# Neighbour sums tile by tile, gate logits with the gate matrix stationary, and one GpSimd split behind a new wait

## The reference, cut to what matters

```python
def _L1_gnn_ref(x, wc, wn, bias, edge_index):      # second layer
    alpha = x @ wc
    beta = x @ wn
    sums = segment_sum(beta[dst], src)
    return alpha + sums / counts[:, None] + bias

def _L2_gnn_ref(x, gate_W, gate_b, Wl, bl, Wr, edge_index):   # third layer
    gates = softmax(x @ gate_W + gate_b)            # 4 experts
    top_v, top_i = top_k(gates, 2)
    # each of 4 experts, two layers:
    #   h = relu(mean_over_neighbours(h) @ Wl[e, l] + bl[e, l] + h @ Wr[e, l])
    # out = the two chosen experts, weighted by their gates
```

## Time and profile before

| what | value |
|---|---|
| median of 3 runs | 498.01 us (497.74 to 500.13) |
| the profiled execution, its own time | 497.47 us |
| its span, first to last instruction | 495.7 us |
| outside the span | 1.8 us |
| PE busy | 458.0 us, 92% |
| DVE busy | 306.9 us, 62% |
| ACT busy | 192.0 us, 39% |
| POOL busy | 164.2 us, 33% |
| chain that ended last, by engine | PE 63%, DVE 20%, issue 6%, POOL 5%, ACT 3%, DVE queue 3% |

### The profile page before, as it was taken

One profiled execution on the slowest core, in us unless ns is written; L12 is line 12 of the kernel. 1 busy time (PEld: TensorE's weight loads), 2 busy tenths in 40 slices (PEclk: granted clock), 3 DMA queues, 4 the chain that ended last, 5 costly groups with the idle time before them and its releaser, 6 DMA issues.

```text
span 495.7 us, 5939 instructions
## 1 busy us (share of the span) xinstructions
PE 458.0 (92%) x2107; PEld 334.1 (67%) x2107; DVE 306.9 (62%) x574; ACT 192.0 (39%) x264; POOL 164.2 (33%) x107
## 2 busy tenths in 40 slices
PE   4999996889869899899899999999999999999996
PEld 2465442334346778678678888888888888888654
DVE  5999836999975994877685333622362237133654
ACT  5888516546130631142441335123422252224232
POOL 3000131112243984448150433443344334343000
PEclk9999999899979999889998999999999999999999
DMA  8750000000030224203220032203420242120002
GB/s 265 202 225 1 1 1 22 0 1 0 1 106 0 72 100 170 85 1 117 77 86 0 19 127 110 86 2 109 161 87 3 91 141 89 41 85 1 0 1 85
DMA packets 22474, 34.34 MB, mean 69 GB/s; under 512 B 5680, under 2 KB 5936, under 8 KB 22448
## 3 DMA queue, kind: packets, MB, share of 16 engines
q1 hardware_dynamic: 22160, 33.85, 20.2%
q10 hardware_dynamic: 288, 0.13, 0.1%
HBM read 32.93 MB, written 1.05 MB: 69 GB/s over the span
## 4 chain that ended last, share of the span: by engine, by line
PE 63%; DVE 20%; issue 6%; POOL 5%; ACT 3%; DVEq 3%; DMA 1%; POOLq 0%
PE ps L1146 16%; PE ps L1148 16%; PE ps L1147 16%; PE ps L1208 4%; DVE one_src L784 3%; PE ps L1174 3%; PE ps L1175 3%; DVE rsum L886 2%; DVEq L784 2%; DVE e_sb L373 2%; DVE stats L713 2%; POOL x_sb L477 1%; PE ps L1287 1%; POOL w_lo L453 1%; PE ps L1159 1%
## 5 line engine op out<-in xcount | busy, mean ns | idle before, releaser
L452 POOL TENSOR_TENSOR w_lo<-w_stage,w_hi 128x1024 fp32r<-128x1024 f32 x22 | 52.7, 2395 | 137.7 <-ACT w_hi L528 137.7
L528 ACT ACTIVATE w_hi<-w_stage 128x2048 fp32r<-128x2048 f32 x23 | 43.9, 1910 | 73.1 <-PE ps L1148 73.1
L453 POOL TENSOR_TENSOR w_lo<-w_stage,w_hi 128x1024 fp32r<-128x1024 f32 x22 | 57.4, 2607 | 0.0
L1146 PE MATMUL ps<-w_hi,hid_hi 128*128 128x512 f32 x128 | 49.8, 389 | 0.0
L1147 PE MATMUL ps<-w_lo,hid_hi 128*128 128x512 f32 x128 | 49.8, 389 | 0.0
L1148 PE MATMUL ps<-w_hi,hid_lo 128*128 128x512 f32 x128 | 49.8, 389 | 0.0
L1063 DVE TENSOR_SCALAR tmp<-ps,bl 128x512 f32<-128x512 f32 x16 | 12.0, 751 | 52.2 <-ACT hid_hi L670 52.2
L1146 PE MATMUL ps<-T_hi,w_hi 128*128 128x512 f32 (+1 forms) x112 | 41.6, 372 | 1.8 <-DVE T_lo L743 1.4
L1148 PE MATMUL ps<-T_hi,w_lo 128*128 128x512 f32 (+1 forms) x112 | 40.7, 363 | 0.0
L1147 PE MATMUL ps<-T_lo,w_hi 128*128 128x512 f32 (+1 forms) x112 | 40.7, 363 | 0.0
L471 POOL TENSOR_TENSOR rstd<-vareps,scalars 128x1 f32<-128x1 f32 x24 | 15.8, 660 | 59.4 <-DVE vareps L715 59.4
(11 more groups left out here) (206 smaller groups left out, 1064.4 us busy)
## 6 DMA issues: line engine op xcount, KB each, us to landing
w_stage<-in_L_gnn_Wr SPq DMA_DIRECT2D x8, 1024.0 KB, 5.3
w_stage<-in_L_gnn_Wl SPq DMA_DIRECT2D x8, 1024.0 KB, 5.2
w_stage<-in_L_gnn_W SPq DMA_DIRECT2D x5, 1024.0 KB, 6.3
x_sb<-in_x SPq DMA_DIRECT2D x4, 256.0 KB, 3.6
w_q<-in_L_gnn_Wq SPq DMA_DIRECT2D x1, 1024.0 KB, 7.8
w_k<-in_L_gnn_Wk SPq DMA_DIRECT2D x1, 1024.0 KB, 10.1
w_v<-in_L_gnn_Wv SPq DMA_DIRECT2D x1, 1024.0 KB, 5.7
w_o<-in_L_gnn_Wo SPq DMA_DIRECT2D x1, 1024.0 KB, 9.6
```

The source lines that it names most:

```text
L452: gp.tensor_tensor(w_lo[s][:, 0:2], stage[s][:, 0:2], f32(w_hi[s][:, 0:2]), ALU.subtract)
L453: gp.tensor_tensor(w_lo[s][:, 2:4], stage[s][:, 2:4], f32(w_hi[s][:, 2:4]), ALU.subtract)\
L528: nc.scalar.activation(w_hi[u % 2][:], stage[u % 2][:], ACT.Copy).then_inc(hi_made, 1)
L1146: nc.tensor.matmul(goal, a_hi, b_hi, start=start, stop=False, **kw)
```

## The change

Three things change, and what they need.

1. The neighbour sums of the second layer are written out in place of the call: for each output tile all eight products k = 0 to 3 in a row, with the branch `If(slow > 0)` ahead of the last pair of each tile, so four branches in place of one.
2. The gate matrix, hi and lo side by side as 8 columns `gw`, becomes the stationary operand and T the moving one: 4 matmuls of T_hi into 8 rows of bank 3 and 4 of T_lo into its first 4 rows. ACT copies the 8 rows to SBUF (`gate_rows`). After the first two banks of expert 0's first product, PE turns them back with 4 matmuls in plain float32: `gate_rows` (8 rows, 128 columns) is stationary, and `fold`, an 8 x 4 matrix that adds the hi and lo rows, moves. DVE makes `fold` at the start by one small addition.
3. POOL waits for `tr_lo` of LN4's last tile before it splits the second expert matrix.

```diff
@@ gpsimd
             split_lo(FIRST_EXPERT)
             rstd_of(LN4)
+            gp.wait_ge(tr_lo, split_no(T4, NT - 1))
             for u in range(FIRST_EXPERT + 1, W_LAST + 1):
                 split_lo(u)
@@ scalar
                 nc.scalar.activation(agg_hi[:, j, :], tmp[:, j, :], ACT.Copy).then_inc(agg_hi_made, 1)
+            act.wait_ge(gate_rows_done, 1)
+            nc.scalar.activation(gate_rows[0:2 * EXPERTS, :], ps[0:2 * EXPERTS, 3, :], ACT.Copy)              .then_inc(gate_rows_out, 1)
             act.wait_ge(gexp_ask, 1)
@@ vector
-            link(nc.vector.tensor_copy(gw_hi[:], gate_w[:]))
-            nc.vector.tensor_tensor(gw_lo[:], gate_w[:], f32(gw_hi[:]), ALU.subtract).then_inc(gate_split, 1)
+            link(nc.vector.tensor_copy(gw_hi, gate_w[:]))
+            nc.vector.tensor_tensor(gw_lo, gate_w[:], f32(gw_hi), ALU.subtract).then_inc(gate_split, 1)
+            nc.vector.tensor_tensor(fold[:], ident[:, 0:EXPERTS], ident[:, EXPERTS:2 * EXPERTS], ALU.add)              .then_inc(gate_split, 1)
@@ tensor
-            sums_over_edges(0, ct_hi, ct_lo, R_hi, R_lo, beta_lo_made, 0, 1, gamma_done)
+            for t in range(NT):
+                for k in range(NT):
+                    if k == NT - 1:
+                        with pe.If(slow > 0):
+                            for kk in range(NT):
+                                nc.tensor.matmul(ps[:, t, :], ct_lo[:, kk, col(t)], R_hi[:, kk, :], start=False,
+                                                 stop=False, skip_group_check=True)
+                    nc.tensor.matmul(ps[:, t, :], ct_hi[:, k, col(t)], R_hi[:, k, :], start=k == 0, stop=False)
+                    last = nc.tensor.matmul(ps[:, t, :], ct_hi[:, k, col(t)], R_lo[:, k, :], start=False,
+                                            stop=k == NT - 1)
+                last.then_inc(gamma_done, 1)
@@ tensor
-            pe.wait_ge(gate_split, 1)
-            for t in range(NT):
-                for k in range(DT):
-                    last = mm3(ps[:, 3, t * EXPERTS:(t + 1) * EXPERTS], T_hi[:, k, col(t)], T_lo[:, k, col(t)],
-                               gw_hi[:, k, :], gw_lo[:, k, :], k == 0, k == DT - 1)
-            last.then_inc(logits_done, 1)
+            pe.wait_ge(gate_split, 2)
+            for k in range(DT):
+                nc.tensor.matmul(ps[0:2 * EXPERTS, 3, :], gw[:, k, :], T_hi[:, k, :], start=k == 0, stop=False,
+                                 skip_group_check=True)
+            for k in range(DT):
+                last = nc.tensor.matmul(ps[0:EXPERTS, 3, :], gw_hi[:, k, :], T_lo[:, k, :], start=False,
+                                        stop=k == DT - 1, skip_group_check=True)
+            last.then_inc(gate_rows_done, 1)
@@ tensor, in the loop over the banks j of an expert's first layer
+                        if n == 0 and e == 0 and j == 2:
+                            pe.wait_ge(gate_rows_out, 1)
+                            for t in range(NT):
+                                last = nc.tensor.matmul(ps[:, 3, t * EXPERTS:(t + 1) * EXPERTS],
+                                                        gate_rows[0:2 * EXPERTS, col(t)], fold[0:2 * EXPERTS, :],
+                                                        start=t == 0, stop=t == NT - 1, skip_group_check=True)
+                            last.then_inc(logits_done, 1)
                         if n == 0 and e == 0 and j == 3:
                             pe.wait_ge(logits_out, 1)
```

More of the change, by code:

```diff
@@ L123, in build @@
     part = place("part", [P, NT, D], F32, rM)
+    gate_rows = place("gate_rows", [P, N], F32, rM)
+    fold = place("fold", [P, EXPERTS], F32, rM + N * 4)
     one_dst = place("one_dst", [P, RING, P], F16, rVZ)
@@ L162, in build @@
     gate_w = little("gate_w", [P, DT, EXPERTS])
-    gw_hi = little("gw_hi", [P, DT, EXPERTS], F32R)
-    gw_lo = little("gw_lo", [P, DT, EXPERTS], F32R)
+    gw = little("gw", [P, DT, 2 * EXPERTS], F32R)
+    gw_hi, gw_lo = gw[:, :, 0:EXPERTS], gw[:, :, EXPERTS:2 * EXPERTS]
     scalars = little("scalars", [P, 2])
@@ L312, in build @@
         gate_split, logits_done, logits_out = sem("gate_split"), sem("logits_done"), sem("logits_out")
+        gate_rows_done, gate_rows_out = sem("gate_rows_done"), sem("gate_rows_out")
         gexp_ask, gexp_done = sem("gexp_ask"), sem("gexp_done")
```

## The result

| | median of the runs | lowest to highest | ratio to before, 95% interval |
|---|---|---|---|
| before | 498.01 us | 497.74 to 500.13 (5 runs) | |
| the change | 495.27 us | 494.05 to 495.71 (5 runs) | 0.9929 [0.9906, 0.9951] |
| the change, again beside other kernels (e5) | 495.34 us | 493.88 to 497.50 (12 runs) | 0.9940 [0.9921, 0.9959] |

The account below looks back on a forecast made before the run. TensorE, gapless from the expert phase on, was taken as the bound, so earlier starts reach the end. 1.60 + 3.62 + 1.55 - 2.0 - 0.81 = 3.96 us less: 498.01 to 494.1 us, range 491.9 to 496.0.

Parts of the forecast that it names:

- The ladder: TensorE's waits for R_lo of each tile, from gamma to the logits: sums' order and moved split together gain 1.60 us.
- The sums tile by tile: Neighbour sums ahead of the first normalisation: R_lo of the first tile 0.34 us earlier, bounds 0 and 1.36.
- That rival: Branches between gamma's tiles stop TensorE's issue; at 2.5 us each the kernel takes 500.5 us; chance 0.04.
- The logits: Gate logits on TensorE: eight matmuls of 512 columns take 1.81 us in place of 5.43, 3.62 gained.
- The new wait: TensorE ahead of bank 2 waits for ACT's copy `gate_rows`, behind `agg_lo` blocked by the split: 2.0 us lost.
- The fold: Four plain-float matmuls ahead of bank 2 that turn the logits back: 0.81 us lost, between 0.4 and 1.0.
- The clock: TensorE's clock was to stay at 1.00 throughout; a fall in the gap ahead of bank 2 had chance 0.12.
- mine lies near the first: The 2.8 us gap ahead of bank 2 resembles an earlier 2.64 us stretch of transposes that stayed at clock 1.00.
- The likeliest case: The whole-kernel forecast: 3.96 us less, 494.1 us, with 493.1 to 494.6 from its unknown sizes; chance 0.60.
- the clock's rival: The clock falls in the gap ahead of bank 2, eight products take 1.55 us more: 495.6 us; chance 0.12.
- The chances: Whole-kernel time: faster than 495.5 us 0.79, within 0.5% 0.16, slower 0.05.

Follow-up runs that it names:

- e5: The change itself, run and profiled once more beside other kernels: 495.34 us, ratio 0.9940.
- e4: The kernel before with only GpSimd's (POOL's) new wait added, so the split of the second expert matrix moves down: 498.31 us, ratio 1.0003.
- e3: The change without GpSimd's new wait, so the split runs at its old place: 493.29 us, ratio 0.9899.
- e7: The kernel before with only the neighbour sums' edit (tile by tile): 497.09 us, ratio 0.9984.
- e6: The kernel before with only the logits' edit: 492.04 us, ratio 0.9872.
- e1: The change with ACT's copy of the logit rows moved from behind the fourth `agg_hi` to behind the second: 491.48 us, ratio 0.9864.
- e2: The change with eight useless matmuls of 512 columns put ahead of TensorE's wait for the copy: 492.80 us, ratio 0.9889.
- e8: e1 with ACT's wait for gamma moved from ahead of the first normalisation to behind it: 489.96 us, ratio 0.9827.
- e10: e8 without GpSimd's new wait, so the split is back at its old place: 491.87 us, ratio 0.9870.
- e11: The change with sixteen useless matmuls of 4 columns ahead of TensorE's wait for the copy: 495.35 us, ratio 0.9939.
- e9: The change with four useless matmuls of 512 columns ahead of TensorE's wait for the copy: 495.37 us, ratio 0.9930.

## Why the prediction was right and where it failed

**The ladder** was right: 1.94 us gained in place of 1.60. Of these the new wait gave 1.6 (e4: 20.67 - 19.09; e3), where the forecast's share was 1.26. The first block came at 9.71 as laid out (9.72); the last two steps were 2.33 and 2.29 instead of 2.47 once R_lo was ready well ahead.

**The sums tile by tile**, 0.34 us: right in size in e7 (0.31 at n = 1), for the reason given, ACT's wait for all four tiles. The queue ahead of the first R_lo went; but e6 shows that it hung on 0.4 us by which DVE starts late in the kernel before, and that beside the logits' edit this order of the sums is worth nothing. The added branches cost nothing: 32 matmuls from 235.29 to 242.32 are 0.227 apart. That rival is out. The small addition that makes `fold` delayed nothing late, as forecast, but it wasn't small: it reads two operands in SBUF beside a split of POOL and lasted 2.42 us (227.41 to 229.83, where POOL's half ends at 229.80). The last addition of alpha still starts 0.20 us after gamma's first matmul, as before.

**The logits** were right: 1.85 us in place of 1.81 (254.02 to 255.87). So these matmuls with 8 and 4 stationary columns start as far apart as those with 128, 0.23 us.

**The new wait** was right: TensorE went on 28.02 us after gamma, forecast 28.33, and waited 1.96 us (263.31 less 261.35, where the next matmul would have started), forecast 2.0. The Trainium skill (SBUF — State Buffer, "Who interferes with whom") says that a VectorE instruction with two SBUF inputs contends with a GpSimd one that reads SBUF, that the port pair they share is an exclusive lock, and that the order of issue decides who blocks; here the trace agrees, with 1.74 and 1.50 us for `agg_lo` where 0.69 is usual.

**The fold** was too cheap: 0.98 us in e1, e2 and e5, where the clock is at 1.00 while it runs, in place of 0.81. In the change's first profile it took 1.25, above the bound of 1.0; the granted clock over these 1.25 us is 0.76: there the fall begins within it, in e5 behind it.

**The clock** is where the forecast failed. The step was "mine lies near the first": I judged the 2.8 us ahead of bank 2 by one stretch in one profile, and gave the fall 0.12 and a price of 1.55 us. It fell in both profiles of the change, for 1.6 and 3.2 us; with the rival's own price, 34.6 + 1.55 = 36.15 us is where e5 has its n = 1. The likeliest case was thus the wrong one (its own span was 493.1 to 494.6 us). The median, 495.27, is that of the clock's rival (495.6), and it lies within the range (491.9 to 496.0) because the range reached to that rival: the number held, the path to it did not. The gap without dense matmuls is the cause: the granted clock is 0.50 behind it in both profiles of the change, and it is 1.00 where the wait is gone (e1, e3, e6, e8, e10) or filled with dense matmuls (e2). The stretch that I compared it with was no safe measure either, for in e11 the clock fell there. The Trainium skill (TensorE: Matmul & The Clock Gate, "Why this matters for your kernels") warns of idle gaps between matmul bursts, but only of gaps longer than this one, a condition that the prediction left out. The traces go against it as a bound: the clock fell behind 1.81 us of idle time in the change and behind 0.91 us in e9's profile.

**The chances**: faster by over 0.5% had 0.79. The median fell 2.74 us, 0.55%, which is just over the bound of 2.5 us; the interval of the ratio, 0.9906 to 0.9951, reaches to just inside half a per cent. With the fall of the clock missed, that the median fell on this side of the bound is in part luck.

## What to carry to other kernels

Moving work out of one queue's way puts it in another's: look which late consumer stands behind the new place, and in which order its engine serves it; here one copy, served two places too late, turned a gain of 1.6 us into a loss of 2. A wait of TensorE costs its length and what the clock loses behind it: here 2.0 us and then 1.6 or 3.2 more. Place a wait that can't be avoided where dense matmuls can cover it. And a stretch that kept its clock in one profile is no proof that it does in each execution.

## What was unexpected of the hardware

- Eight useless dense matmuls in a gap made the kernel 2.5 us faster (492.80 against 495.34).
- Sixteen matmuls of 4 columns in the same gap (e11) didn't keep the clock, although TensorE was busy; nor did 48 in e4, where the clock was at 0.50 while the last 15 ran. Eight of 512 columns on 8 and 4 stationary columns, with dense work behind, came with no fall in e1.
- The same kernel's executions differ in how long the clock stays low (7 and 13 slow matmuls), and, as it seems, in whether it falls: e9's runs spread over 5.1 us, those of e8, with no such wait, over 1.2. (The runs of the kernel before, whose clock falls behind its thin logits, spread over 4 us or so in each group.)
- Ahead of gamma, the change's first profile was 1.2 to 1.3 us faster than those of before and of e5, with granted clock 0.94 from 205 to 235 us, where the others had 0.89: of the 2.2 us by which the change's first profile is shorter than that of before, 1.2 are of this kind and not of the edit.
